# A graph network kernel: a fifth group of nodes is sorted, ranks come every 4 blocks, and one-hots compare with one operand

## The reference

```python
# part 0: three graph convolutions, degrees from both ends
h   = x * out_norm[:, None]
agg = segment_sum(h[src], dst, num_segments=12500) * in_norm[:, None]
x   = elu(agg @ W + b)                      # three times
x1  = layernorm(x_in + x)
# part 1: one GIN layer with edge attributes
msg = relu(x1[src] + edge_attr @ W_edge.T + b_edge)
h   = (x1 + segment_sum(msg, dst)) @ W1.T + b1
h   = relu(gamma * (h - mean) * rsqrt(var + eps) + beta) @ W2.T + b2
out = layernorm(x1 + h)
```

## Time and profile before

| | |
|---|---|
| median of 3 runs | 6527.94 us |
| the profiled execution | 6538.76 us |
| its span | 6537.0 us |
| TensorE busy | 5427.9 us, 83% |
| VectorE busy | 4686.0 us, 72% |
| GpSimd busy | 3555.2 us, 54% |
| mean granted TensorE clock | 0.927 |

### The profile page before, as it was taken

The page is one execution under the profiler, slowest core; times in us unless marked ns, Lnnn a source line. Parts: engine busy times, 40 slices in busy tenths (PEclk is TensorE's granted clock), DMA queues, the critical chain, the costliest instruction groups (busy, mean ns, idle before and its releaser), DMA issues.

```text
span 6537.0 us, 110254 instructions
## 1 busy us (share of the span) xinstructions
PE 5427.9 (83%) x37560; PEld 3239.1 (50%) x37561; DVE 4686.0 (72%) x17501; ACT 2240.6 (34%) x3807; POOL 3555.2 (54%) x3787
## 2 busy tenths in 40 slices
PE   5899997889987899999999998777777777777773
PEld 4456665556654454555555544444444444444442
DVE  4777789999999754555555545777777777666664
ACT  1777776777542100000001112333333332222221
POOL 7411112223110167777777676777777777777770
PEclk9999999999999999999999999888888888777875
DMA  2522223333220499989989994222222222222210
GB/s 80 216 102 82 82 106 115 117 136 115 84 80 31 160 283 281 282 278 278 282 276 285 284 294 126 41 41 41 41 41 41 41 41 39 39 39 39 39 37 21
DMA packets 420909, 823.11 MB, mean 126 GB/s; under 512 B 146377, under 2 KB 247909, under 8 KB 413525
## 3 DMA queue, kind: packets, MB, share of 16 engines
q1 hardware_dynamic: 292324, 708.34, 33.3%
q0 software_dynamic: 113632, 82.11, 6.7%
q10 hardware_dynamic: 14400, 25.61, 1.4%
HBM read 620.48 MB, written 195.25 MB: 125 GB/s over the span
## 4 chain that ended last, share of the span: by engine, by line
PE 40%; POOL 29%; DVE 14%; issue 11%; ACT 4%; PEld 1%; DMA 1%; PEldq 0%; ACTq 0%; POOLq 0%; DVEq 0%
POOL rows_f L1048 28%; PE banks L2093 22%; DVE rows_f L1302 9%; PE banks L2015 7%; PE banks L1977 5%; ACT wide L1780 3%; DVE rows_f L1299 3%; PE banks L1984 2%; PEld banks L2093 1%; PE banks L2068 1%; PE banks L2075 1%; PE banks L2041 1%; PE banks L2325 1%; POOL tmp L924 1%; POOL hid L926 1%
## 5 line engine op out<-in xcount | busy, mean ns | idle before, releaser
L1048 POOL DMA_INDIRECT rows_f<-table,src_key x1875 | 1804.2, 962 | 571.3 <-issue 571.2
L1013 POOL DMA_INDIRECT sorted_recs<-onehot,rows x1280 | 1234.4, 964 | 601.7 <-issue 379.3
L1780 ACT ACTIVATE wide<-banks 128x784 fp8e4<-128x784 f32 x1563 | 1256.4, 825 | 738.2 <-PE banks L2015 734.8
L1302 DVE TENSOR_SCALAR rows_f<-rows_f,tmp 128x392 f16<-128x392 f16 (+2 forms) x5625 | 1415.9, 327 | 126.3 <-PE banks L2015 118.9
L2015 PE MATMUL banks<-rows_f 128*128 128x392 f16 (+1 forms) x6656 | 1238.8, 307 | 132.3 <-DVE rows_f L1302 124.0
L968 POOL DMA_INDIRECT onehot<-edge_runs_dram,rows_f x352 | 383.0, 1088 | 1454.6 <-DVE onehot L1156 1310.4
L2093 PE MATMUL banks<-wide,rows_f 128*128 128x512 fp8e4 (+1 forms) x4900 | 1126.7, 375 | 12.8 <-issue 12.8
L2015 PEld LDWEIGHTS banks<-rows_f 128*128 128x128 f16 x6656 | 859.4, 146 | 439.7 <-issue 163.1
L2182 PE MATMUL banks<-w_edge_blk,rows 80*128 80x320 f32 x750 | 344.5, 546 | 671.6 <-DVE rows_f L1602 661.8
L1977 PE MATMUL banks<-wide,onehot 128*128 128x392 fp8e4 x3125 | 793.8, 334 | 106.8 <-ACT wide L1780 98.3
L1394 DVE SCALAR_TENSOR_TENSOR onehot<-banks,onehot 128x98 f16<-128x98 f32 (+2 forms) x996 | 264.6, 266 | 513.5 <-PE banks L2075 504.4
(11 more groups left out here) (328 smaller groups left out, 6582.0 us busy)
## 6 DMA issues: line engine op xcount, KB each, us to landing
wide<-counts SPq DMA_DIRECT2D x504, 896.0 KB, 5.9
counts<-wide SPq DMA_DIRECT2D x50, 3136.0 KB, 10.5
rows_f<-table,src_key POOLq DMA_INDIRECT x1875
sorted_recs<-onehot,rows POOLq DMA_INDIRECT x1280
sorted_recs<-rows SPq DMA_DIRECT2D x24, 640.0 KB
rows<-attr_dram SPq DMA_DIRECT2D x375, 40.0 KB
agg_a<-attr_dram ACTq DMA_DIRECT2D x50, 250.0 KB
agg_b<-attr_dram ACTq DMA_DIRECT2D x50, 250.0 KB
```

What stands on the lines that cost most here:

```text
L1013: G.indirect_dma_start(out=sorted_recs[:, :], out_offset=bass.IndirectOffsetOnAxis(ap=row_of[:, t:t + 1], axis=0), in_=taken[g % 2][:, n * ...
L1048: G.indirect_dma_start(out=g_rows[:, n % ROW_RING, k, :], out_offset=None, in_=table32[:, :], in_offset=bass.IndirectOffsetOnAxis(ap=src_k ...
L1302: last = V.tensor_scalar(key, iota_key[:, 0:item.width * BLOCKS], key_cols[:, n:n + 1], None, ALU.is_equal)
L1780: A.activation(win_counts[o.half % 2][:, :, d0:d0 + o.quads * QUAD].rearrange("p b (q c) -> p b q c", c=QUAD), counted, ACT.Copy, scale=UN ...
```

## The change

The fifth window of 512 nodes is sorted too. That makes 1430 tiles to rank and write (1280), 294 chunks (245, 49 more of 6 tiles), 345 units (375) and so 1725 fetches (1875), and 491 buckets (393). A rank turn comes after every 4 blocks, 24 in a step (19). The load of granule g stands one step of counts earlier, after each 3.75 pieces (3.94), and the granules left at the end are loaded after all counts and ahead of the last rows of the node table. The 1430 keys no longer fit one tile and stand in two. The zeroed rows that are filled beforehand take 29 DMAs (25), 6 in a turn (5). In the edge loop the base is taken off the destinations beforehand, so that each one-hot compares `iota` with one column.

```diff
-SORTED = 4
+SORTED = 5
-RANK_EVERY = 5
+RANK_EVERY = 4
-RANK_NODES, RANK_LATE = 5, 14
+RANK_NODES, RANK_LATE = 7, 17
-FILLS = 25
-TAKE_RATE = RANKED // GRAN / ((len(DENSE) - 3) * PIECES)
+KEYS_A = 1280
+FILLS, FILLS_A_TURN = -(-BUCKET_ROW[SORTED] * RECORD // P // KEYS_A), 6
+TAKE_EVERY = 3.75
...
-                    if m >= 2 and taken_now < RANKED // GRAN and taken_now <= ((m - 2) * PIECES + k) * TAKE_RATE:
+                    if m >= 1 and taken_now < RANKED // GRAN and taken_now * TAKE_EVERY <= (m - 1) * PIECES + k:
                         take_records(taken_now)
...
+            for g in range(taken_now, RANKED // GRAN):
+                take_records(g)
             for i in range(WINDOWS - 3, WINDOWS):
                 store_rows(i)
...
-                V.tensor_scalar(keys, keys, float(BUCKETS - 1), None, ALU.min).then_inc(s_lims, 1)
+                V.tensor_scalar(keys_b, key_sum[:, KEYS_A:], float(BUCKETS - 1), None, ALU.min)
+                V.tensor_scalar(keys_a, key_sum[:, 0:KEYS_A], float(BUCKETS - 1), None, ALU.min).then_inc(s_lims, 1)
...
-                    V.tensor_copy(c_dst[:, s, 0:tiles], ints[:, :, EDIM + 1]).then_inc(s_prep, 1)
+                    V.tensor_scalar(c_dst[:, s, 0:tiles], ints[:, :, EDIM + 1], -float(c.w * WIN), None, ALU.add).then_inc(s_prep, 1)
...
-                        last = V.tensor_scalar(g_hot[:, n % HOT_RING, k, :], iota_win[:, 0:UNIT_NODES], g_base[:, n // 2:n // 2 + 1],
-                                               dst_key[:, t:t + 1], ALU.add, ALU.is_equal)
+                        last = V.tensor_scalar(g_hot[:, n % HOT_RING, k, :], iota_win[:, 0:UNIT_NODES], dst_key[:, t:t + 1], None, ALU.is_equal)
...
-                        last = dst_hot(c_hot[:, s, k, :], c.w, c_dst[:, s, k:k + 1])
+                        last = V.tensor_scalar(c_hot[:, s, k, :], iota_win[:, :], c_dst[:, s, k:k + 1], None, ALU.is_equal)
...
+                gathered = dst_key[:, FIRST_UNIT * UNIT:].rearrange("p (g t) -> p g t", t=GRAN)
+                link(V.tensor_tensor(gathered, gathered, g_base.rearrange("p (g o) -> p g o", o=1).to_broadcast([P, len(BASES), GRAN]), ALU.subtract))
```

More of the change, by code:

```diff
@@ L478, in gnn_kernel, with keys_of @@
         rows16_f = rows16[:, :, :, :].rearrange("p s k n -> p (s k n)").bitcast(F32)
-        keys, row_of = rows16_f[:, 0:RANKED], rows16_f[:, 0:RANKED].bitcast(I32)
+        keys_a, keys_b = rows16_f[:, 0:KEYS_A], hid_row[:, BLOCKS * P // 2:BLOCKS * P // 2 + RANKED - KEYS_A]
         key_i = feat_row[:, 0:RANKED].bitcast(I32)
-        key_hi = feat_row[:, RANKED:2 * RANKED]
+        key_hi, key_sum = feat_row[:, RANKED:2 * RANKED], feat_row[:, 2 * RANKED:3 * RANKED]
+        def keys_of(a, b):
+            return keys_a[:, a:b] if b <= KEYS_A else keys_b[:, a - KEYS_A:b - KEYS_A]
         hots = HOTS - 2
@@ L660, in gnn_kernel @@
         s_put, PUT0 = s_near[2:4], [16 * (b - a) for a, b in SETS[2:4]]
+        PUT_END = [PUT0[s] + 16 * GRAN * len(range(s, RANKED // GRAN, 2)) for s in range(2)]
         s_take, TAKE0 = [s_load, s_w], [32, 16 * (6 * LAYERS + 2 + CHUNK_TILES + 6)]
@@ L783, in _ @@
                     sp.wait_ge(s_zero, 3)
-                if 2 <= n < 2 + FILLS // 5:
-                    for k in range(5):
-                        fill((n - 2) * 5 + k)
+                if n >= 2:
+                    for k in range((n - 2) * FILLS_A_TURN, min((n - 1) * FILLS_A_TURN, FILLS)):
+                        fill(k)
                 done += sum(o.half == half for o in OCTETS)
@@ L1012, in put_records @@
                             t = (g * 2 + n) * UNIT + k
[L1013 removed]
+                            G.indirect_dma_start(out=sorted_recs[:, :], out_offset=bass.IndirectOffsetOnAxis(ap=keys_of(t, t + 1).bitcast(I32), axis=0),
                                                  in_=taken[g % 2][:, n * UNIT + k, :], in_offset=None).then_inc(s_put[g % 2], 16)
@@ L1225, in edge_bounds @@
                 link(V.tensor_scalar(key_i, key_i, WIN.bit_length() - 1, None, ALU.logical_shift_right))
-                link(V.tensor_copy(keys, key_i))
+                link(V.tensor_copy(key_sum, key_i))
                 link(V.tensor_scalar(key_i, src_key[:, 0:RANKED], P.bit_length() - 1, None, ALU.logical_shift_right))
                 link(V.tensor_copy(key_hi, key_i))
-                link(V.scalar_tensor_tensor(out=keys, in0=keys, scalar=float(BLOCKS), in1=key_hi, op0=ALU.mult, op1=ALU.add))
-                V.tensor_scalar(keys, keys, float(BUCKETS - 1), None, ALU.min).then_inc(s_lims, 1)
+                link(V.scalar_tensor_tensor(out=key_sum, in0=key_sum, scalar=float(BLOCKS), in1=key_hi, op0=ALU.mult, op1=ALU.add))
+                V.tensor_scalar(keys_b, key_sum[:, KEYS_A:], float(BUCKETS - 1), None, ALU.min)
+                V.tensor_scalar(keys_a, key_sum[:, 0:KEYS_A], float(BUCKETS - 1), None, ALU.min).then_inc(s_lims, 1)
             def set_bounds():
@@ L1377, in bucket_hots @@
                     a, b = rank_columns(t)
-                    V.tensor_scalar(bucket_hot[t % HOTS][:, 0:b - a], iota_win[:, a:b], keys[:, t:t + 1], None, ALU.is_equal).then_inc(s_bhot, 1)
+                    V.tensor_scalar(bucket_hot[t % HOTS][:, 0:b - a], iota_win[:, a:b], keys_of(t, t + 1), None, ALU.is_equal).then_inc(s_bhot, 1)
             done = [0]
@@ L1394, in rank_to @@
                     V.scalar_tensor_tensor(out=ranked[:, t % 2, 0:b - a], in0=rank_ps[t % STREAMS][:, a:b], scalar=1.0, in1=bucket_hot[t % HOTS][:, 0:b - a],
-                                           op0=ALU.mult, op1=ALU.mult, accum_out=keys[:, t:t + 1]).then_inc(s_rowf, 1)
+                                           op0=ALU.mult, op1=ALU.mult, accum_out=keys_of(t, t + 1)).then_inc(s_rowf, 1)
                     bucket_hots(t + AHEAD)
@@ L1398, in rank_to @@
                         dve.wait_ge(s_rowf, ROWF0 + t + 1)
-                        unit = slice(t + 1 - UNIT, t + 1)
-                        V.tensor_scalar(row_of[:, unit], keys[:, unit], float(SORTED_ROWS - 1), 0.0, ALU.min, ALU.max).then_inc(s_rowi, 1)
+                        unit = keys_of(t + 1 - UNIT, t + 1)
+                        V.tensor_scalar(unit.bitcast(I32), unit, float(SORTED_ROWS - 1), 0.0, ALU.min, ALU.max).then_inc(s_rowi, 1)
                     done[0] += 1
@@ L1572, in sorted_edge_sums @@
             def sorted_edge_sums():
-                def dst_hot(out, w, column):
-                    return V.tensor_scalar(out, iota_win[:, :], win_base[:, w:w + 1], column, ALU.add, ALU.is_equal)
                 def prepare(j):
```

11 lines of the change are left out of this document (5 added, 6 removed).

## The result

The changed kernel takes 6448.17 us (median of 4 runs, 6445.34 to 6450.83) against 6526.81 us (4 runs, 6524.89 to 6528.27) of the kernel before on the same chip: a ratio of 0.988, 95% interval 0.9863 to 0.9897, or 79 us less. The forecast was 6416. Its profiled execution took 6450.82 us, with a span of 6449.1 us.

A forecast was written before the change was run, and what follows sets the result against it. GpSimd's queue of fetches was taken to bound the edge loop, TensorE the dense stage. Fetches starting 77.5 us later and taking 190.1 less gave -112.6: 6426 profiled, 6416 us median; 8-in-10 range 6396 to 6466.

The forecast's parts named there:

- The fetches' part: Edge loop: 30 units, 150 fetches fewer on GpSimd at 1.267 us each, 190.1 us less.
- the start of the fetches: After GpSimd's writes: 1430 writes end at 4079, so fetches start at 4080, 77.5 us later than before.
- The 10 us by which my reckoning fell short for the kernel before: End of writes: the same reckoning ended 10 us before the true 3972.8, so 4069 was raised to 4079.
- the offset: Whole program: profiled execution taken as 10.8 us above the median, as before, turning 6426 into 6416 us.
- The cover: Dense stage: TensorE's part grows 15 to 20 us, ending near 4010, hidden by GpSimd's work until 4079; 69 us of cover.
- "a few us" for pieces behind a take: Dense stage's first steps: SyncE waits at granule loads with counts queued behind, so TensorE may lose a few us, hidden.
- The loads: Dense stage: record loads come every 13.1 us, GpSimd needs one each 12.64, so loads pace it from granule 58 until ranks end.
- The edge loop: Per unit TensorE needs 5.5 us, VectorE 5.7, or 4.9 with one operand; GpSimd's 6.334 stays the bound.
- A: Rival, dense stage: writes wait for landings, 13.1 us per granule, writes end at 4133, time 6470; chance 0.09.
- B: Rival, edge loop: TensorE or VectorE becomes the bound, 6.6 us per unit in the first half, +46 us, 6462; chance 0.08.
- C: Rival, edge loop: TensorE enters cold; at clock 0.65 it needs 7.36 us per unit, +354 us, 6770; chance 0.04.

The follow-up runs named there:

- The run with 3.5: The changed kernel with records taken every 3.5 pieces of the counts instead of every 3.75: 6474.5 us, ratio 0.992 to the kernel before.
- three-of-five run: The changed kernel with only 3 of 5 tiles of each edge-loop unit fetched, the others' part left out of the result: 5961.5 us, ratio 0.9133.
- the one pair of runs where the bound was taken away: The changed kernel with 3 of 5 tiles per unit fetched, slow DMA: 7286.0 us with one-operand one-hots, 7366.7 us with two-operand ones.
- the two runs with five fetched: The changed kernel with records taken every 3.6 pieces, and the same with rank turns from the first step's block 40, slow DMA: 8198.0 and 8159.6 us.

## Why the prediction was right, and where its numbers were off

**Right by its mechanism.** The fetches' part, 190.1 us, came out as 4002.5 to 6376.9 against 4102.1 to 6287.8: 188.7. The first write was due at 2257 and came at 2256.5. A step with ranks was 24.5 us and is 24.6 (ScalarE's copies). GpSimd's idle time of 28.75 us is gone, and what is late next is GpSimd itself. The one-hots were priced at nothing; they cost 5 us here and 8 us on the kernel before.

**The term that was mis-sized: the start of the fetches, 4080 for 4102.1.** The result lies 32 us above the forecast. The profiled time was reckoned at 6426 and is 6450.8: 22 us of that at this start, 1.4 in the fetches and 1.1 in the tail. The writes were to take 1430 x 1.264 = 1807.5 us and 14.5 us more for loads. They took 1844.7. Two things make up these 37.2 us. The price of a write is 0.967 + 0.305 = 1.272 us; I had rounded the gap to 0.30 and taken the duration 3 ns short, 12 us over 1430. And the gaps over 0.4 us hold 25.6 us, of which 7.6 behind late records and 18.0 in pauses; I had expected 14.5 for late records and no pauses. The pauses could be seen in the trace of before: its writes' "issue" idle, 379.3 us, stands over 1190 gaps by its source view, 0.319 us each, and not the fetches' 0.305. I had carried the gap of the fetches over to the writes, though their own row was there. The 10 us by which my reckoning fell short for the kernel before I put down to long steps; nine pauses of 16.4 us in all stand in its writes.

**The other 8 us are the offset.** I took the median 10.8 us below the profiled execution, as it was before. After, the two differ by 2.7 us.

**The cover.** The dense stage's end went from 3993.5 to 4022.7, 29 us and not 15 to 20. The last two steps took 24.0 and 15.3 us where before they took 22.4 and 12.0, and TensorE waited 9.6 us for counts. All of it lay under the cover. That was 70 us, and not the 78 between last copy and last write, as the first fetch could not have started sooner than 9 us after the copy. The run with 3.5 shows what the prediction's "a few us" for pieces behind a take are worth when the takes really bite: 91 us.

**The loads.** I had GpSimd paced by them from the 58th granule on. In fact it was itself slower, by its true price and the pauses, and met late records only at six granules, from the 74th on.

**The edge loop.** VectorE was reckoned at 4.9 us per unit where chunks have 8 tiles, and is busy 410.51 / 500 x 6.34 = 5.2 there. The reason is the saving per one-hot: it was 0.061 us at 224 wide as said (0.063), but 0.036 at 512, where the same was assumed and 0.27 us were expected for 0.306. That the three-of-five run makes 4.87 per unit is no proof of the 4.9: it is an average with the lighter second half in it. With two operands I had 5.7, under 6.334, so GpSimd would stay the bound: it did. TensorE was to rise to some 85% and rose to 79% (393 of 500 us). Its clock rose from 0.87 to 0.94, where the forecast held it, and 5.5 x 0.87 / 0.94 = 5.1 us per unit would be 80%. So the page of the Trainium skill that the prediction weighed, "VectorE: DVE Perf Modes", section "The TRN2 errata", whose price has no term for a scalar column, is not borne out: a second column costs time at both widths.

**The rivals.** A: the writes did not wait for landings. With a take every 3.5 pieces SyncE stands at a take until its buffer is free, and still no write waited for records: the landing of the writes and the load together fit in the other buffer's 12.7 us. B: VectorE never held GpSimd, whose gaps are all "issue". C: TensorE did go cold, 0.63 from 4001 to 4102, and was at 0.94 in the loop's first half.

## What to carry to other kernels

Count the transfers of a queue over the whole kernel before crediting a change with taking some of them out of one loop: what a change that moves work along a saturated engine can bring is the idle time of that engine that it fills, here 98 us, and not the 190 us by which the one loop grows shorter. Then look at which of two streams ends last at the junction (here last write or last dense output), and tune until both end together; past that point each us gained on one is lost on the other. A part of the change that serves an engine off the path is measured apart before it is called useful: it cost 5 to 8 us here, and brought 81 us in the one pair of runs where the bound was taken away (with the slow DMA).

## What the runs showed that I had not expected

- GpSimd's indirect writes paused for up to 3.7 us behind the 113th, 223rd and so on, at most every 110th, with the DMA engines 0.82 to 0.91 busy; the 1725 to 2045 fetches at a share of 0.2 show no such pause. At a share of 0.82 to 0.85 the pauses of the changed kernel hold 18.0 us, and at 0.91, in the kernel before, 16.4. Where the share was 0.75 to 0.79 they hold 1.5, 7.5 and 12.3 us, and with the slow DMA (0.55) none stands at these places in the two runs with five fetched. So they go with a fixed count of transfers and not with the records. What they are stays open.
- When takes are issued sooner, SyncE's order costs TensorE 91 us for 7% more frequent takes.
- With two fifths of the fetches gone and VectorE at 98%, the remaining ones took 1.014 us on average and not 0.963, at the same median of 0.944; 240 of 1035 were longer than 1.1 us, 239 of them across that same operation of VectorE.
